# Three fp32r products for the gate and the retention's query product in a fused fp32 decoder step kernel

## The reference, cut to what matters

```python
# 1. retention block (Wq, Wk, Wv are 8 blocks of 32x32)
xn  = layernorm(x)
q, k, v = xn*Wq, xn*Wk, xn*Wv                    # per head
ret = norm_per_head(((q k^T) * decay) v) * gn_w + gn_b
gated = xn @ W1
x = x + (gated * sigmoid(gated) + ret) @ W2
# 2. cross attention, 16 heads, causal, keys and values from ctx
x = x + softmax(mask(qh kh^T)) vh @ Wo + bo      # qh from layernorm(x)
# 3. feed-forward with 8 experts, two sequences each
x = x + gelu(layernorm(x) @ w1[e] + b1[e]) @ w2[e] + b2[e]
```

## Time and profile before

| | us |
|---|---|
| median of 3 runs | 371.97 (371.9 to 372.0) |
| the profiled execution's own time | 369.38 |
| its span, first to last instruction | 367.6 |
| PE busy | 338.3 (92%) |
| PEld busy | 280.1 (76%) |
| DVE busy | 254.6 (69%) |
| ACT busy | 238.9 (65%) |
| POOL busy | 163.5 (44%) |

### The profile page before, as it was taken

How to read it: one execution, slowest core, us unless ns; L and a number is a source line. 1 busy time by engine, 2 the same in 40 slices (tenths; PEclk the granted TensorE clock), 3 DMA queues, 4 the chain that set the end, 5 groups by cost and what they waited for, 6 DMA issues and landing times.

```text
span 367.6 us, 8998 instructions
## 1 busy us (share of the span) xinstructions
PE 338.3 (92%) x3283; PEld 280.1 (76%) x3299; DVE 254.6 (69%) x555; ACT 238.9 (65%) x586; POOL 163.5 (44%) x148
## 2 busy tenths in 40 slices
PE   7878679999999999999999999999999998989697
PEld 3657457987789877987789867987789866858596
DVE  5674786677766976677775976678765966482974
ACT  4552663776756866677847766677848764787551
POOL 4237150364615366363625457362634550445340
PEclk9999999999999999999999999999999999999999
DMA  5940102022031400413023400404014300013300
GB/s 151 307 172 1 31 2 107 37 62 85 1 112 78 144 0 17 171 33 110 0 66 120 143 0 14 169 7 137 0 47 141 116 6 10 30 16 116 116 29 30
DMA packets 22314, 26.97 MB, mean 73 GB/s; under 512 B 2896, under 2 KB 20112, under 8 KB 22288
## 3 DMA queue, kind: packets, MB, share of 16 engines
q1 hardware_dynamic: 21472, 26.52, 22.3%
q10 hardware_dynamic: 816, 0.10, 0.2%
HBM read 24.51 MB, written 2.10 MB: 72 GB/s over the span
## 4 chain that ended last, share of the span: by engine, by line
PE 77%; DVE 9%; issue 7%; ACT 4%; POOL 1%; DMA 1%; ACTq 0%; DVEq 0%; POOLq 0%
PE c L1208 22%; PE a L1208 16%; PE b L1208 14%; PE b1k L1344 7%; PE b1k L1208 6%; PE b2k L1208 4%; DVE negmax L912 2%; PE c L1371 2%; ACT prob L596 1%; ACT probT L558 1%; PE a L1223 1%; DVE scD L893 1%; PE b2k L1223 1%; DMA wk_c<-in_L_attn_Wk 1%; PE a L1301 1%
## 5 line engine op out<-in xcount | busy, mean ns | idle before, releaser
L460 POOL TENSOR_TENSOR w_lo<-w_in,w_hi 128x512 fp32r<-128x512 f32 x32 | 40.8, 1305 | 30.4 <-ACT w_hi L558 26.3
L596 ACT ACTIVATE prob<-b,negmax 128x128 f32<-128x128 f32 x124 | 36.1, 398 | 25.4 <-DVE negmax L912 25.4
L1344 PE MATMUL b1k<-ident,prob 128*128 128x128 f32 x256 | 40.0, 279 | 9.3 <-ACT probT L558 4.5
L466 POOL TENSOR_TENSOR w_lo<-w_in,w_hi 128x512 fp32r<-128x512 f32 x28 | 35.5, 1287 | 28.6 <-ACT w_hi L558 26.8
L453 POOL TENSOR_TENSOR rstA<-varA,minus_half 128x16 f32<-128x16 f32 x8 | 23.4, 2927 | 49.2 <-DVE varA L1047 49.2
L1344 PEld LDWEIGHTS b1k<-ident,prob 128*128 128x128 f32 x256 | 28.1, 140 | 17.3 <-ACT prob L596 7.2
L558 ACT ACTIVATE w_hi<-w_in 128x512 fp32r<-128x512 f32 x64 | 39.1, 653 | 2.6 <-PE b L1208 2.6
L1208 PE MATMUL c<-xTC_hi,w_hi 128*128 128x256 f32 x108 | 31.8, 294 | 0.8 <-DVE xTC_lo L862 0.8
L919 DVE COPY probT<-b1k 128x512 f32<-128x512 f32 x32 | 22.0, 687 | 13.1 <-PE b1k L1344 13.0
L1208 PE MATMUL c<-w_hi,h_hi 128*128 128x256 f32 x96 | 30.8, 321 | 0.1
L1208 PE MATMUL c<-xTC_lo,w_hi 128*128 128x256 f32 x108 | 30.5, 282 | 0.0
(11 more groups left out here) (301 smaller groups left out, 1110.4 us busy)
## 6 DMA issues: line engine op xcount, KB each, us to landing
w_in<-in_L_ffn_w SPq DMA_DIRECT2D x16, 1024.0 KB, 5.6
x_in<-in_x SPq DMA_DIRECT2D x8, 256.0 KB, 2.8
c_in<-in_ctx SPq DMA_DIRECT2D x8, 256.0 KB, 2.9
out<-x2b SPq DMA_DIRECT2D x7, 256.0 KB, 2.2
b_cur<-in_L_ffn_b SPq DMA_DIRECT2D x8, 128.0 KB, 3.0
W_sb<-in_L_attn_W SPq DMA_DIRECT2D x2, 256.0 KB, 4.2
decay_sb<-in_decay SPq DMA_DIRECT2D x1, 512.0 KB, 3.8
h_in<-in_L_xattn_Wk SPq DMA_DIRECT2D x1, 256.0 KB, 4.3
```

The costliest lines, as they stand in the source:

```text
L460: pool.tensor_tensor(w1_lo[:, :, part], w1_in[:, :, part], w1_hi[:, :, part].bitcast(F32), ALU.subtract).then_inc(s_w1lo, 1)
L466: pool.tensor_tensor(w2_lo[:, part, :], w2_in[:, part, :], w2_hi[:, part, :].bitcast(F32), ALU.subtract).then_inc(s_w2lo, 1)
L596: ins = nc.scalar.activation(prob[:, u % PR, g, :], score_banks[u][:, g * P:(g + 1) * P], ACT.Exp, bias=negmax[:, u, g:g + 1], scale=-1.0)
L1344: ins = nc.tensor.transpose(b1k[:, g * P:(g + 1) * P], prob[:, u % PR, g, :], ident[:, :])
```

## The change

x of the retention is kept in three forms for every step but the first: xTA in fp32 as before (scores and values still read it), xTA_hi (rounded, by a second ACT copy out of a0 that stands ahead of the copy into xTA), and xTA_lo (the rest, xTA - xTA_hi, by DVE: `split_x`, both inputs in SBUF, 128x512). `split_x` stands behind `probT_odd(7)` and ahead of the statistics of x1; in iteration 0 it stands behind those statistics. POOL makes W1_hi, qk_hi, W1_lo and qk_lo once, ahead of its first iteration. The gate and the query product become three fp32r products each from step 1 on. Gate piece 0 also waits for xTA_lo and for the weights.

```diff
--- before.py
+++ after.py
@@ -87,6 +87,10 @@
         wv_bd = sb("wv_bd", [P, C, P])
         qk_bd = sb("qk_bd", [P, C, P])
         W1_sb = sb("W1_sb", [P, C, D])
+        W1_hi = sb("W1_hi", [P, C, D], F32R)
+        W1_lo = sb("W1_lo", [P, C, D], F32R)
+        qk_hi = sb("qk_hi", [P, C, P], F32R)
+        qk_lo = sb("qk_lo", [P, C, P], F32R)
         W2_sb = sb("W2_sb", [P, C, D])
         gn_sb = sb("gn_sb", [P, 2, C])
         xWq_hi = sb("xWq_hi", [P, C, D], F32R)
@@ -115,6 +119,8 @@
         rsA = sb("rsA", [P, NB])
         xnA = sb("xnA", [P, NB, D])
         xTA = sb("xTA", [P, C, T])
+        xTA_hi = sb("xTA_hi", [P, C, T], F32R)
+        xTA_lo = sb("xTA_lo", [P, C, T], F32R)
         qA = sb("qA", [P, C, T])
         thA = sb("thA", [P, C, T])
         silA = sb("silA", [P, C, T])
@@ -237,6 +243,10 @@
         s_keep = signal("s_keep")
         s_TA = signal("s_TA")
         s_xTA = signal("s_xTA")
+        s_xTAhi = signal("s_xTAhi")
+        s_xTAlo = signal("s_xTAlo")
+        s_Whi = signal("s_Whi")
+        s_Wlo = signal("s_Wlo")
         s_qA = signal("s_qA")
         s_qsb = signal("s_qsb")
         s_gA = signal("s_gA")
@@ -550,6 +560,15 @@
             for j in range(RJ):
                 rows = slice(RD * j, RD * (j + 1))
                 pool.tensor_scalar(wv_bd[rows, :, rows], wv_c[rows, :, :], 1.0, None, ALU.mult).then_inc(s_wvbd, 1)
+            pool.wait_ge(s_wvbd, RJ)
+            pool.wait_ge(s_W1, 16)
+            pool.wait_ge(s_qkc, 1)
+            wait_apart(pool)
+            for w, hi in ((W1_sb, W1_hi), (qk_bd, qk_hi)):
+                pool.tensor_scalar(hi[:, :, :], w[:, :, :], 1.0, None, ALU.mult).then_inc(s_Whi, 1)
+            pool.wait_ge(s_Whi, 2)
+            for w, hi, lo in ((W1_sb, W1_hi, W1_lo), (qk_bd, qk_hi, qk_lo)):
+                pool.tensor_tensor(lo[:, :, :], w[:, :, :], hi[:, :, :].bitcast(F32), ALU.subtract).then_inc(s_Wlo, 1)
             pipeline(pool, body)
 
         @block.scalar
@@ -812,6 +831,8 @@
 
             def transposed_x(step):
                 act.wait_ge(s_TA, step + 1)
+                if later(step):
+                    copy(xTA_hi[:, :, :], a0[:, :].rearrange("p (c t) -> p c t", c=C), s_xTAhi)
                 copy(xTA[:, :, :], a0[:, :].rearrange("p (c t) -> p c t", c=C), s_xTA)
 
             for dst, src, s_load in ((wq_c, Wq, s_wq), (wk_c, Wk, s_wk), (wv_c, Wv, s_wv)):
@@ -856,6 +877,12 @@
                 for b in range(NB):
                     nc.vector.tensor_scalar(xn[:, b, :], src[:, b, :], mv[:, b, 0:1], rs[:, b:b + 1],
                                             ALU.subtract, ALU.mult).then_inc(s_xn, 1)
+
+            def split_x(step):
+                dve.wait_ge(s_xTAhi, step)
+                dve.wait_ge(s_xTA, step + 1)
+                nc.vector.tensor_tensor(xTA_lo[:, :, :], xTA[:, :, :],
+                                        xTA_hi[:, :, :].bitcast(F32), ALU.subtract).then_inc(s_xTAlo, 1)
 
             def split_transposed(s_hi, step, bank, hi, lo, s_lo):
                 dve.wait_ge(s_hi, step + 1)
@@ -1152,8 +1179,11 @@
                 if do_b:
                     divide(0)
                     probT_odd(7)
+                    split_x(a + 1)
                 dve.wait_ge(s_x1, a + 1)
                 statistics(a, x1, statB, mvB, s_lnB)
+                if not do_b:
+                    split_x(a + 1)
                 if do_b:
                     divide(1)
                     split_transposed(s_cTB, a, b1k, cTB_hi, cTB_lo, s_cTBlo)
@@ -1279,7 +1309,11 @@
 
                 def ret_queries():
                     for k in range(C):
-                        ins = mm(a1[:, k * T:(k + 1) * T], qk_bd[:, k, :], xTA[:, k, :])
+                        out = a1[:, k * T:(k + 1) * T]
+                        if later(a):
+                            ins = mm_split(out, (qk_hi[:, k, :], qk_lo[:, k, :]), (xTA_hi[:, k, :], xTA_lo[:, k, :]))
+                        else:
+                            ins = mm(out, qk_bd[:, k, :], xTA[:, k, :])
                     ins.then_inc(s_qA, 1)
 
                 def retention(bank):
@@ -1668,10 +1702,18 @@
             def gate(step, piece):
 
                 m, k = piece // C, piece % C
+                cols = slice(m * P, (m + 1) * P)
                 if piece == 0:
                     pe.wait_ge(s_xTA, step + 1)
-                ins = mm(a0[:, m * T:(m + 1) * T], W1_sb[:, k, m * P:(m + 1) * P], xTA[:, k, :],
-                         start=(k == 0), stop=(k == C - 1))
+                if not later(step):
+                    weights, x_parts = (W1_sb,), (xTA,)
+                else:
+                    weights, x_parts = (W1_hi, W1_lo), (xTA_hi, xTA_lo)
+                    if piece == 0:
+                        pe.wait_ge(s_Wlo, 2)
+                        pe.wait_ge(s_xTAlo, step)
+                ins = mm_split(a0[:, m * T:(m + 1) * T], [w[:, k, cols] for w in weights], [t[:, k, :] for t in x_parts],
+                               start=(k == 0), stop=(k == C - 1))
                 if piece == C * C - 1:
                     ins.then_inc(s_gA, 1)
```

## The result

Median of 20 runs: 373.38 us (372.11 to 375.83), beside 371.68 us (369.13 to 372.28) for 20 runs of the kernel before. The ratio is 1.0065, with an interval of 1.0046 to 1.0084: slower by 1.7 us. Forecast were 373.6 us and 371.1 to 375.0.

A forecast was written before the change was run, and what follows sets the result against it. PE, with 77% of the chain, was taken to bound the kernel, except in round trips through other engines. Terms -1.0 + 2.6 + 0 = +1.6 us on the median of 371.97 gave 373.6 us, range 371.1 to 375.0.

The forecast's parts named there:

- The subtraction is held by POOL: In iterations 2 to 6 DVE's xTA_lo waits on POOL's x2b: about 1.35 us, against 0.69 in 0 and 1.
- What it costs on PE: Iterations 2 to 6: the held subtraction makes DVE's reciprocal late, 0.4, 0.7 and three times 0.5, 2.6 us more.
- PE's road: From the subtraction through gate piece 0 and pvT's transposes to the reciprocal: shorter than DVE's; alone it would cost 1.8 us.
- Gate pieces 0 to 2: End of an iteration: their 0.24 us saving a step only lengthens PE's wait for att, so 0.
- Query products 0.16 us a step: Opening of an iteration, ahead of the wait for qA: two products save 0.16 us, 1.0 us over iterations 2 to 7.
- ACT's copy and POOL's start: ACT's extra 0.60 us copy and POOL's four new instructions, 3.8 to 5.1 us, are hidden in idle time.
- Iteration 0: Subtraction fits DVE's wait for rsB, nothing for xnB; later gates cost 0.2, queries return 0.16: taken 0, bounds -0.1 and +0.2.
- The clock's rival: At the start PE rests before gate pieces 0 to 2, then 2.3 us of work takes twice as long: 375.9 us; chance 0.08.
- The sum: All terms, -1.0 for products, +2.6 for the held subtraction, 0 at the start: +1.6 us, added to the median of before.

The follow-up runs named there:

- experiment 3: Changed kernel with gate and query products back in plain fp32, PE waiting for no part, the parts still made: 373.65 us, ratio 1.0083 to the kernel before.
- 11: Changed kernel with spare PE products filling the rests in iterations 0, 1 and 9, POOL's x2b left where it was: 371.20 us, ratio 1.0022 to the kernel before.
- 10: Changed kernel with POOL's x2b moved ahead of the rests of w1, and spare PE products in iterations 0, 1 and 9: 368.80 us, ratio 0.9952.
- Experiment 5: Changed kernel with gate pieces 0 to 2 in plain fp32 without a wait, PE waiting ahead of the query products instead: 372.53 us, ratio 1.0044.
- experiment 6: Changed kernel with the two query products in plain fp32 again: 374.34 us, ratio 1.0076 to the kernel before.
- 9: Kernel before the change with eight spare PE products in iteration 1 and eight in iteration 9: 369.41 us, ratio 0.9970 to it unfilled.
- experiment 2: Changed kernel with ten spare PE products ahead of gate piece 0 of step 1, in iteration 0: 372.30 us, ratio 1.0045 to the kernel before.

## Why the prediction was right, point by point

- **The subtraction is held by POOL: right, and shown.** 1.32 to 1.40 us in iterations 2 to 6, forecast about 1.35; its end 0.56 us behind POOL's, forecast 0.54 from the earlier trace rows; 0.69 in iterations 0 and 1. The port rule that the Trainium skill gives ("SBUF — State Buffer", section "SBUF: two separate sides") agrees: 1.40 us beside L490, 0.68 once POOL has another order. As it is worded there, for any instruction of GpSimd that reads SBUF, these traces do not bear it out, and they decide: in the kernel before, a DVE subtraction of two 128x512 SBUF tiles took 0.68 us in the middle of a POOL power of 128x16 elements, the same as with POOL at rest (L1038 at 22.51), and another 0.69 us (h_lo, at 120.65) beside a one-input copy of 128x512 (L513, 119.53 to 121.08). The forecast also read too much into the trace where it said that no two-input DVE instruction ran beside L480: L974 did, at 353.61, in 0.42 us, like att of the same size; it has one input in PSUM and one in SBUF, so it says nothing on two from SBUF.

```profile
18.96 2.90 POOL L453 TENSOR_TENSOR rstA<-varA,minus_half 128x16 f32<-128x16 f32 x1 [0.23 <-DVE varA L1047]
19.39 0.68 DVE L1038 SCALAR_TENSOR_TENSOR xWv_lo<-h_in,xWv_hi 128x512 fp32r<-128x512 f32 x1
```

- **What it costs on PE: right in sum.** It acts through the reciprocal (experiment 3), and PE's wait for a part need not be there; that PE's road is the shorter one was not so (they end together). Forecast 2.6 us for iterations 2 to 6; kernels 11 and 10 differ by 2.40 in the median and by 2.18 in these five periods. By iteration it is 0.49, 0.29, 0.52, 0.47 and 0.41 us, where 0.4, 0.7 and three times 0.5 stood. Less idle time before the reciprocal was to mean more loss, but iteration 3, with only 0.46 us, lost least. Part of that lies in kernel 10, whose iteration 3 is 0.16 us longer than its iteration 4. Why is open.
- **Gate pieces 0 to 2 are worth nothing: right.** Experiment 5 has the period of the changed kernel.
- **Query products 0.16 us a step: somewhat too high.** The time on PE is right (1.06 us for queries and piece 3, forecast 1.06), but only 0.11 of it reaches the period (experiment 6). Kernels 10 and 9 differ by 0.50 us over iterations 2 to 6, 0.10 each. With -0.18 in iteration 1 the six iterations give -0.68, where -1.0 was forecast. Of the 0.61 us between the medians, the traces show +0.23 from step 0 to step 1, these -0.68, and next to nothing behind step 7, so 0.45; the traced execution of number 10 is the slowest of its 12.
- **ACT's copy and POOL's start: right.** POOL's four instructions run from 9.97 to 14.34 us (4.4 us, bounds 3.8 and 5.1), and it idles 2.04 us before silA.
- **Iteration 0: the step that failed, by 0.22 us.** I wrote "nothing for xnB" and took 0, with bounds -0.1 and +0.2. Counted from step 0, step 1 begins after 21.97 to 21.99 us instead of 21.74 to 21.76 with the clock held; without the saving of the query products (experiment 3) it is 22.13, so they do give the forecast 0.16 back there, of 0.39. The subtraction starts at 28.76, and POOL's rsB, which takes 0.71 us in the loop, starts at 28.93 and takes 1.08: here DVE came first and POOL was held, until 0.56 us behind DVE's end at 29.45. The three traces without the subtraction have 0.70 us for this rsB, all ten with it 1.08. So xnB came at 30.04 and not at 29.60. I had asked only who holds DVE, not whom DVE holds.
- **The clock's rival (0.08) happened as well**, as it was written: PE rests ahead of the gates and the queries run at the lower level. The price was about 1 us, not 2.3 (33.37 against 32.38 in experiment 2): gate pieces 0 to 2 still ran mostly at the higher level, and I had doubled all of the work. The Trainium skill ("TensorE: Matmul & The Clock Gate", section "Why this matters for your kernels") warns against idle gaps of PE; the trace agrees: this rest, 2.83 us, was followed by the lower level.
- **Why the median was still met.** The sum was +1.6, the clean cost is 1.79, and the medians differ by 1.70. The sum is near because its errors cancel: from step 0 to step 7, kernels 11 and 9 differ by 2.17 for the hold (forecast 2.6), -0.68 for the products (-1.0) and +0.23 for the start (0), 1.72 in all. The median is a second matter. I added the change to the median of before as if the rest of the difference stayed the same, and had not seen that the kernel before too loses clock, in most executions. The commonest mean clock is 0.991 in both (11 of 20 runs after, 373.39 us; 35 of 84 before, 371.77), and there they differ by 1.6. But at 0.995 they differ by 2.1 (5 runs after, 372.40; 25 before, 370.29), no run after reached 1.00, and beside the batches of before with medians of 370.37 and 370.15 the difference would have been 3.0 and 3.2 us. That the 20 runs of before shown with the result were mostly at 371.6 to 372.3 is luck, and so is part of the agreement. Compared profile with profile, the change costs 5.1 us of span; with the clock filled in both it is 2.0 (369.5 less 367.5), so about 3 are clock that the profiled execution of before had not lost.

## What to carry to other kernels

A new instruction on an engine with slack is priced by what runs on its neighbour at that very moment: look for the two-input SBUF instructions of DVE and POOL that would overlap, in both directions, and set their order so that they don't. Put a saving where the engine that gets faster is followed by itself; ahead of a round trip it only lengthens a wait. When one profiled execution stands well under the median, compare the granted clock of its stretches with other runs before a sum is made against it.

## What the runs showed of the hardware

- The hold works both ways and ends about 0.56 us behind the end of the first instruction, of either engine: DVE's 128x512 subtraction went from 0.69 to 1.40 us behind POOL's two-input addition of 128x512, and POOL's 128x2 power from 0.70 to 1.08 us behind DVE's subtraction. It is not the same for every pair: behind POOL's 128x16 power, and beside its one-input copy, the same kind of DVE subtraction took 0.68 and 0.69 us. No run tells what in the instruction makes the difference.
- PE's clock fell not only after a full rest (2.83 us) but also in iteration 1, where PE was busy 2.19 of 5 us in many short pieces, and in some executions only. Twenty-six spare products, in places where PE waited anyway, gave a mean granted clock of 0.999 or 1.00 in all 12 runs of kernel 10, and took a spread of 3 us down to 0.4.
- At the full clock a 128x256 fp32 product costs PE 0.43 us and three fp32r products of parts 0.35 us; at the lower level a record of the same fp32r product comes every 0.21 us instead of every 0.12.
